# Causal layer: SyncE instead of ScalarE issues the transfers of the row maxima into the score operand

## What is computed

```python
qkv = einsum('ble,fe->blf', layernorm(x), w_in)
q, k, v = split into 16 heads of 16 features
scores = einsum('bhqd,bhkd->bhqk', q, k) * scale + alibi_bias      # -inf above the diagonal
attn = softmax(scores)
x = x + (attn @ v, heads joined) @ w_out.T
x = x + ffn(layernorm(x))
```

## Time and profile before

| | |
|---|---|
| median of three runs | 3670.48 us |
| the profiled execution | 3654.36 us, span 3652.6 us |
| TensorE busy | 3445.5 us, 94% |
| VectorE, ScalarE, GpSimd busy | 79%, 68%, 58% |
| DMA engines, packets of SyncE's queue (q1) | 53.6% of 16 engines over the span |
| packets of ScalarE's queue (q10) | 0.4%, 2048 packets, 2.10 MB |
| layer 2 alone | from about 1830 us to the end |

### The profile page before, as it was taken

One profiled execution on the slowest core, in us unless ns is written; L12 is line 12 of the kernel. 1 busy time (PEld: TensorE's weight loads), 2 busy tenths in 40 slices (PEclk: granted clock), 3 DMA queues, 4 the chain that ended last, 5 costly groups with the idle time before them and its releaser, 6 DMA issues. The chain is left out here.

```text
span 3652.6 us, 79167 instructions
## 1 busy us (share of the span) xinstructions
PE 3445.5 (94%) x26824; PEld 1944.6 (53%) x26824; DVE 2870.9 (79%) x8451; ACT 2482.7 (68%) x5347; POOL 2114.2 (58%) x2340
## 2 busy tenths in 40 slices
PE   5999999999999999999689999999999999999997
PEld 2444444444444444444446666666666666666664
DVE  5899999999998989999266777777777777776772
ACT  2788888788888878887345666666666666665663
POOL 2367777677767767775744455455555555454542
PEclk7999999999999999999789999999999999999997
DMA  4344434434443444344465767768767767767660
GB/s 122 70 82 85 95 69 90 93 86 78 84 99 72 88 88 90 74 84 94 87 134 96 135 120 127 128 119 134 134 121 127 135 120 127 135 120 127 120 109 25
DMA packets 251933, 376.44 MB, mean 103 GB/s; under 512 B 21930, under 2 KB 122448, under 8 KB 251264
## 3 DMA queue, kind: packets, MB, share of 16 engines
q1 hardware_dynamic: 249484, 369.28, 53.6%
q10 hardware_dynamic: 2048, 2.10, 0.4%
HBM read 223.97 MB, written 136.95 MB: 99 GB/s over the span
## 5 line engine op out<-in xcount | busy, mean ns | idle before, releaser
L681 DVE TENSOR_REDUCE maxima<-ps_max 128x1 f32<-128x512 f32 x2048 | 1274.3, 681 | 96.2 <-PE ps_max L444 91.4
L1523 DVE CUSTOM_DVE_ANT_0 ps_max<-ps_max,mask 128x512 f32<-128x512 f32 (+3 forms) x2048 | 962.1, 515 | 352.5 <-PE ps_max L1245 350.0
L575 ACT ACTIVATE probs<-ps_rest 128x512 f32<-128x512 f32 x2048 | 1074.0, 603 | 225.0 <-PE ps_rest L457 222.4
L1396 ACT ACTIVATE probs<-ps_rest 128x512 f32<-128x512 f32 (+3 forms) x2048 | 773.3, 437 | 451.6 <-PE ps_rest L1266 399.3
L444 PE MATMUL ps_max<-k_op,q_op 48*128 48x512 f32 x2048 | 723.9, 446 | 61.6 <-DVE maxima L681 53.3
L457 PE MATMUL ps_rest<-q_op,k_op 50*128 50x512 f32 x2048 | 717.0, 441 | 0.3
L444 PEld LDWEIGHTS ps_max<-k_op,q_op 48*128 48x128 f32 x2048 | 339.8, 186 | 531.8 <-DVE maxima L681 411.1
L1245 PE MATMUL ps_max<-k_op,q_op 51*128 51x512 f32 (+3 forms) x2048 | 562.3, 365 | 22.9 <-DVE maxima L1523 3.1
L1266 PE MATMUL ps_rest<-q_op,k_op 53*128 53x512 f32 (+3 forms) x2048 | 557.9, 365 | 21.0 <-DMA q_op<-mrows 21.0
L478 PE MATMUL ps_pv<-probs,v_op 128*32 128x512 f32 x4096 | 542.2, 605 | 1.0 <-ACT oT L587 1.0
L1245 PEld LDWEIGHTS ps_max<-k_op,q_op 51*128 51x128 f32 x2048 | 314.4, 187 | 165.5 <-DVE maxima L1523 87.6
(11 more groups left out here) (145 smaller groups left out, 5462.6 us busy)
## 6 DMA issues: line engine op xcount, KB each, us to landing
qk_parts<-qparts SPq DMA_DIRECT2D x192, 512.0 KB, 3.2
q_op<-qk_parts SPq DMA_DIRECT2D x384, 256.0 KB, 8.0
k_op<-qk_parts SPq DMA_DIRECT2D x192, 256.0 KB, 10.6
xin<-in_x SPq DMA_DIRECT2D x32, 512.0 KB, 4.5
xres<-in_x SPq DMA_DIRECT2D x32, 512.0 KB, 5.6
x_mid<-xo SPq DMA_DIRECT2D x32, 512.0 KB, 3.2
xin<-x_mid SPq DMA_DIRECT2D x32, 512.0 KB, 7.1
xres<-x_mid SPq DMA_DIRECT2D x32, 512.0 KB, 15.6
```

Source lines behind the costliest of these rows:

```text
L575: act.activation(probs[:, quad % 2, at:at + S], ps_rest[:, bank("exp", b, p), :], ACT.Exp).then_inc(ps_out["exp"], 1)
L681: dve.tensor_reduce(at, ps_max[:, bank("max", c, k), :], AX.X, ALU.max).then_inc(ps_out["max"], 1)
L1396: act.activation(probs[quad % 2][:, at:at + nq], ps_rest[:, bank("exp", b, p), 0:nq], ACT.Exp).then_inc(ps_out["exp"], 1)
L1523: dve.tensor_tensor_reduce(row, row, mask[:, S - keys:S], 1.0, LOWEST, ALU.add, ALU.max, at).then_inc(ps_out["max"], 1)
```

## The change

`send_maxima` moves, unchanged, from ScalarE's program to SyncE's, and the word `send` in the plan is taken by SyncE instead of ScalarE. The plan's text is the same.

```diff
@@ sync
+        def send_maxima(c, par, quad):
+
+            if not valid(c):
+                return
+            sp.wait_ge(ps_out["m"], c * NQUAD + quad + 1)
+            rows = HALF_ROWS * (quad // 2) + KA
+            first = QUAD * (quad % 2)
+            for r in range(M_ROWS):
+                sp.dma_start(q_op[rows + r:rows + r + 1, par, first:first + QUAD, :].bitcast(F32),
+                             mrows[r:M_ROWS * QUAD:M_ROWS, quad % 2, :].bitcast(F32)).then_inc(m_loaded, 16)
+
@@ body of sync
+                elif kind == "send":
+                    send_maxima(b + d, (par + d) % 2, k)
@@ scalar
-        def send_maxima(c, par, quad):
-
-            if not valid(c):
-                return
-            act.wait_ge(ps_out["m"], c * NQUAD + quad + 1)
-            rows = HALF_ROWS * (quad // 2) + KA
-            first = QUAD * (quad % 2)
-            for r in range(M_ROWS):
-                act.dma_start(q_op[rows + r:rows + r + 1, par, first:first + QUAD, :].bitcast(F32),
-                              mrows[r:M_ROWS * QUAD:M_ROWS, quad % 2, :].bitcast(F32)).then_inc(m_loaded, 16)
-
@@ body of scalar
-                elif kind == "send":
-                    send_maxima(b + d, (par + d) % 2, k)
```

## The result

The changed kernel takes 4365.69 us (median of four runs, 4354.66 to 4371.73) against 3667.95 us for the kernel before. The ratio is 1.192, with a 95% interval of 1.189 to 1.195. The forecast of 4442 us was 76 us too high. Both places and the stalls there came as forecast; the reason given for one of them did not hold. The profiled execution took 4371.73 us.

A forecast was written before the change was run, and what follows sets the result against it. The prediction took TensorE to bound layer 2. It summed 453 + 203 + 148 - 22 - 10 = 772 us onto the profiled 3654.4 us, plus 16 us for the median, giving 4442 us, range 4250 to 4570 us.

The forecast's parts named there:

- The bound and the mechanism: Layer 2: TensorE bounds it, and whatever makes it wait is added to the time one for one.
- Quad 2: Send behind `load_op:1:1` lands with the end of the six loads; 15.1 us in 30 batches, 453 us.
- Quad 3: Send behind `store_qk:0:2`, which waits for GpSimd; 7.0 us in 29 batches, 203 us.
- The clock: TensorE's slow clock after stalls at quads 2 and 3; 2.5 us for each of 59 stalls, 148 us.
- The gains: Waits at quad 1 and slow clock behind them gone, 22 us; ScalarE's idle time before exponentials given back to TensorE, 10 us.
- first rival: At quad 2 the sends do not queue behind the loads; 7.8 instead of 15.1 us, total 4223 us; chance 0.12.
- The clock does not stay low between the stalls: Rival: clock does not recover between quads 2 and 3; net 4 us a batch, 4560 us; chance 0.10.
- Not slower: Rival: SyncE's list runs far enough ahead to issue `load_operands` before quad 2's maxima are ready; 3608 to 3650 us; chance 0.03.

The follow-up runs named there:

- e1: Changed kernel with the send of quad 2 moved ahead of `load_op:1:1` in SyncE's list; 3886.45 us, ratio 1.062.
- e2: Changed kernel with `store_qk:0:2` moved behind the send of quad 3 in SyncE's list; 4125.51 us, ratio 1.127.
- e4: Changed kernel with the send of quad 2 behind the wait of `load_op:1:1` but ahead of its six loads; 3947.51 us.
- e3: Changed kernel with quad 2's send ahead of `load_op:1:1` and `store_qk:0:2` behind quad 3's send; 3620.63 us, ratio 0.989; again 3623.60 us.
- e5: Changed kernel with the send of quad 2 behind two of the six loads of `load_op:1:1`; 4133.03 us.
- e10: Kernel before, all sends on ScalarE, with SyncE holding the loads of `load_op:0:1` until quad 1's send is issued; 3635.08 us, ratio 0.990.
- e9: Kernel before with ScalarE's quad 2 send just ahead of pair 32 and waiting until SyncE has issued the sixth load; 4136.47 us, ratio 1.130.
- e6: Kernel before with ScalarE's send of quad 2 as late as its program allows, just ahead of pair 32; 3857.23 us.
- e7: Kernel before with only the send of quad 1 moved to SyncE, ahead of `load_op:0:1`; 3624.84 us, ratio 0.992.

## Why the prediction was right, and where not

**The bound and the mechanism.** Right. TensorE bounds layer 2, and the two stalls a batch of 14.3 and 6.5 us are what the change costs, with none at quads 0 and 1. e1 and e2 show each by itself, at 3886 and 4126 us.

**Quad 2**, 15.1 us in 30 batches. The rows show about 14.3, and e2 has 425.2 us there from 1900 us on. Part of the difference I had named: I took the difference of two starts, which is about 0.4 us more than the idle time. Together with quad 3 the forecast was 453 + 203 = 656 us, and the page has 639.5. It left out one place of each kind at the joint, and both stalls came there too.

**Quad 3**, 7.0 us against 6.5 in the row shown and 6.0 in the mean of e1 (178.6 us in 30). The lesser of my two readings (6.6) was right. TensorE starts 2.65 us after the issue of the sends, and the 512 KB store 0.4 us ahead of them hardly holds them back, as against 2.5 us in e4.

**The clock**, 148 us. Here e3 is the measure, with the same program but for the stalls: busy 3557.1 against 3425.8 us is 131 us for 62 stalls (e3 has one of that size), 2.1 us each instead of 2.5. The length of the stall does not matter much here: e5, with waits of about 6 instead of 14 us at quad 2, has 3557.2 us.

**The gains**, 22 + 10 us. The former waits go, 21.0 us on the page of the kernel before, and by e3 3445.5 - 3425.8 = 20 us of busy time go too, and not 5. So 41 instead of 22. I had reckoned the slow clock for the long waits alone. Short ones cost it too: e4 has 28 waits more than e1, of about 1.8 us, and 3528.9 against 3509.6 us of busy time, 0.7 us for each. But ten waits at that price are 7 us, and e10, which has the former waits no more, has 3439.3 us, only 6 less than before; where the rest of e3's 20 us comes from stays open. The 10 us that I gave to ScalarE are neither shown nor refuted, as said above. The rest of TensorE's idle time fell by 13 us from before to the changed kernel, from causes that I did not part.

By the profiled executions the sum is 717 instead of 772 us. Of the 55 us that were too many, the idle time at the two places takes 17, the clock after it 17, the former waits 19 and the rest of the idle time 3. The other 22 us of the miss are the 16 us that I added for the median and the 6 us by which the profiled execution lay above the median this time. All these terms made the forecast too high. Only the number of stalls, 62 instead of 59, went the other way, so the total is not right by errors that cancel. The stated bounds, simply added, give 4292 to 4620 us; the 4340 to 4560 of the prediction is narrower and does not say how it was combined.

**The step that failed** is the reason given for quad 2. I took the end of the loads "because the store's 8.5 against 3.2 us shows that one transfer waits for earlier ones of its own queue". It showed only that a transfer waits for earlier ones. With the first rival I set the bound from ScalarE's packets, which went through in 5.6 us "beside 93.6% of load on the other queue", and held the passing of queues for possible. e9 shows none behind six loads. I had misread too: the 5.6 us are the window that I chose, and within it ScalarE's packets started only after 4.1 us, when most of what SyncE had issued before was through. That send came through sooner than one behind six loads because what was ahead of it moved at 292 instead of 114 GB/s, not because it had its own queue. The size was right since on either reading the sends land with the last load.

I also drew the wrong conclusion from the Trainium skill. "DMA: Bandwidth & Descriptors", section "Issuing engines are not separate DMA queues", says that issuing from several engines saves only the sequencer's time. e9 against e2 (4136 and 4126 us) agree with it. But it does not make the move cheap, as I had it in the first rival: behind six loads both queues are equally slow, and then the place in the program is what counts. The turns between queues, which the section "Queues, rings and completion order" of the same page describes, gave the send on the idle queue no visible advantage behind six loads: 12.8 us in e9, and 12.0 us on SyncE's queue.

**The rivals.** That the sends pass the loads is refuted by the changed kernel and by e5. The clock does not stay low between the stalls either: it was 0.97 from 2914 to 2918 us and 0.98 from 2938 to 2942. "Not slower" needed the last load to land before pair 32; it landed 14 us after.

## What to carry to other kernels

A small transfer that a bound engine waits for must be issued before the large ones that nobody needs yet. In these runs it mattered little which engine issued it, and a lot how long the transfers issued just before it still took: hardly at all behind a store of 512 KB, by 10 us behind six loads of 256 KB. So when a transfer moves to another engine's list, place it anew: ahead of every entry there whose own wait ends later than the transfer is ready, and ahead of every burst of loads. Two words moved in the plan turned a loss of 19% into a gain of 1.1%.

## What the runs showed of the hardware that I had not expected

A send of two times 8 KB on ScalarE's otherwise empty queue took 12.8 us to reach TensorE when SyncE had issued six loads of 256 KB just before it, as against 12.0 us on SyncE's own queue. With nothing ahead it takes 2.5 us. The packet counts of e9 show that at least 10.5 of the 12.8 us pass before the send's first packet; what holds the packets back was not tried.

It is not a strict order. Beside the first load, on the other queue, a send took 8.05 us, and on SyncE's own queue with two loads ahead 6.7 us. From 2796.0 to 2801.2 us, in that batch of e6, the send's packets ran among those of the loads:

```profile
q1 hardware_dynamic: 378, 0.69, 104.5%
q10 hardware_dynamic: 16, 0.02, 2.7%
```

So loads issued after a send can delay it too when they come from another queue. In e6 a send issued 0.79 us ahead of the first load took 5.5 us to reach TensorE, and one issued 1.60 us ahead 2.5 us. At quad 1 of the kernel before, the send goes out on ScalarE's queue behind the first of SyncE's six loads and ahead of the others; where TensorE waited for it from 2300 us on, it had taken 10.9 to 15.5 us, and e7 and e10, which send first, have no such waits. That this is also why the runs of the kernel before spread more (49 us, those of e7 19) fits but is not shown.
